# Attention in a perceiver block: narrow broadcast products for the inverse sums, and a minimum per chunk for the scores

## The chip, the cores and the metric

The kernel runs on one core of a Trainium2 chip. The metric is the device time of one execution in microseconds; the table below gives the median of several.

## What is computed

Cross attention with 16 heads of depth 32, then a quantised recurrent layer and a mixture of 8 experts, each on a layer-normalised input with a residual. The change lies in the attention:

```python
q = _split_heads(query_antecedent @ Wq, h) * d_head ** (-0.5)
k = _split_heads(memory_antecedent @ Wk, h)
v = _split_heads(memory_antecedent @ Wv, h)
logits = jnp.einsum('bhqd,bhkd->bhqk', q, k) + bias
weights = jax.nn.softmax(logits, axis=-1)
x = jnp.einsum('bhqk,bhkd->bhqd', weights, v)
```

There are 4 batches of 128 queries and 2048 keys, and one bias map of 128 x 2048 for all heads. The queries carry a factor of -1, so the kernel works with negated logits: it adds a negated bias, takes the least of each row, and raises exp(least - x).

## The kernel before, in words

Heads are worked in quads of four: quad n has batch n // 4, and four quads make a batch, counted here from the first to the fourth. A quad has eight slots, two per head. In a slot TensorE makes two score chunks of 128 x 512 (`score`, L482) in three PSUM banks used in turn (0, 1, 2), so a score waits until the addition three chunks before it has emptied its bank. VectorE empties it (`add_bias`, L712): one instruction adds the bias, writes the sum to `prob`, and keeps the row's minimum. The profile shows it as two rows, the custom instruction and a short one that reads the accumulator into `top`. The second to fourth chunk of a head start from the minimum of the chunk before, and so wait for it. After the fourth, ScalarE raises the whole head of 128 x 2048 to its exponential and sums it (`raise_head`, L894).

Two slots behind, TensorE transposes the exponentials of the quad before, by pairs of key tiles (`turn_pair`, L502, eight transposes a pair, banks 3 and 4 or 5 and 6 by turns). ScalarE copies most pairs out of PSUM (`move_pair`, L902), VectorE the rest (L722): pair 3 and 7 of a quad, and 6 in the third. Every second slot TensorE multiplies two finished pairs by the values (`multiply_pair`, L517), with products 32 columns wide that use four column tiles of its array. A transpose waits until the pair two before it, which had its banks, has been copied.

The order on each engine is written out by hand. On ScalarE the exponential of head j stands at the start of slot 2(j+1), ahead of that slot's copy. On VectorE in slot 3 stand `finish` (L746, the product of the attended values with the inverse sums of the quad two before) and `spread_sums` for the quad before; in slot 5, after its copy of a pair, `copy_sums`.

For the inverse sums VectorE takes reciprocals of the four sums (L728), repeats each 32 times into a 128 x 128 tile (L732), TensorE transposes that tile (`turn_sums`, L527), and VectorE copies it back (L738). The first quad of a batch runs beside the last projections of keys and values; after the fourth there is a tail with the remaining pairs and no scores, then the next batch's projections. GpSimd and the DMA queue of SyncE prepare the stacked keys of later heads.

The core of the addition before:

```python
if c:
    dve.wait_ge(*biased.at(n, j, c - 1))
dve.wait_ge(*scored.at(n, j, c))
dve.tensor_tensor_reduce(
    prob[:, slot, keys], psum[:, scores.of[n, j, c], :], biasmap[:, keys], 1.0,
    top[:, h, (c + 1) % 2:(c + 1) % 2 + 1] if c else HIGHEST, ALU.add, ALU.min,
    top[:, h, c % 2:c % 2 + 1]).then_inc(*biased.made(n, j, c))
```

Of the kernel before, what the change touches and what calls it, by code (L numbers as in the profile page):

```python
# [9 lines left out]
F32 = mybir.dt.float32  # L10
# [4 lines left out]
ALU = mybir.AluOpType  # L15
ACT = mybir.ActivationFunctionType
AX = mybir.AxisListType

P = 128
B = 4  # L20
D = 512
DT = D // P
KEYS = 2048
HEADS = 16
DH = D // HEADS
QUAD = P // DH
# [15 lines left out]
HIGHEST = 3.0e38  # L42
# [7 lines left out]
UNITS = KEYS // CHUNK  # L50
HALVES = 2
HALF = KEYS // HALVES
SLOTS_OF_QUAD = QUAD * HALVES
# [80 lines left out]
def perceiver_block(nc, a, out):  # L134
    with ExitStack() as life:
        def sb(name, shape, dt, stack=life):
            return stack.enter_context(nc.sbuf_tensor(name, shape, dt))
# [4 lines left out]
        def events(name, keys, by=1):  # L142
            return Events(sem(name), list(keys), by)

        psum = life.enter_context(nc.psum_tensor("psum", [P, 8, BANK], F32))


        ident = sb("ident", [P, P], F32)
        region_bias = ExitStack()
        biasmap = sb("biasmap", [P, KEYS], F32, region_bias)  # L150
# [17 lines left out]
        region_kv, region_f, region_r = ExitStack(), ExitStack(), ExitStack()  # L168
# [24 lines left out]
        prob = sb("prob", [P, PS, KEYS], F32, region_r)  # L193
        qstack = sb("qstack", [P, 2, QUAD, P], F32R, region_r)
        oT = sb("oT", [P, P], F32, region_r)
        probT = sb("probT", [P, 2, 2 * QUAD * P], F32, region_r)
        top = sb("top", [P, HEADS, 3], F32, region_r)
        rinv = sb("rinv", [P, 2, QUAD], F32, region_r)
        inverse = sb("inverse", [P, P], F32, region_r)
        region_r.close()  # L200
# [55 lines left out]
        def stack_landed(n, j):  # L256
# [28 lines left out]
        keys_high_g = events("keys_high_g", [(n, j) for n in quads if n % DT for j in range(QUAD)])  # L285
        keys_low_v = events("keys_low_v", [n for n in quads if n % DT == 0])
        keys_low_g = events("keys_low_g", [n for n in quads if n % DT])
        scored, biased = (events(name, [(n, j, c) for n in quads for j in range(QUAD) for c in range(UNITS)])
                          for name in ("scored", "biased"))
        raised = events("raised", [(n, j) for n in quads for j in range(QUAD)])  # L290
        def by_vector(n, p):

# [3 lines left out]
        turned, multiplied = events("turned", pairs), events("multiplied", pairs)  # L296
        moved_v = events("moved_v", [(n, p) for n, p in pairs if by_vector(n, p)])
        moved_a = events("moved_a", [(n, p) for n, p in pairs if not by_vector(n, p)])
        spread_out = events("spread_out", quads)
        sums_turned, sums_copied = events("sums_turned", quads), events("sums_copied", quads)  # L300
        weighted = events("weighted", quads)
        weights_summed = events("weights_summed", WINDOWS)
# [17 lines left out]
        def step_of_slot(n, i):  # L320

            t = SLOTS_OF_QUAD * (n % DT - 1) + i - TURN_LATER
            return t if t >= 0 else None
# [27 lines left out]
        def prob_slot(n, j):  # L351
            return (QUAD * n + j) % PS
# [47 lines left out]
        def tensor_attention(pe):  # L400
# [121 lines left out]
            def turn_sums(n):  # L522
                w, free = (scores.take(("sums", n), sums_copied.at(n)) if n < QUADS - 1 else
                           (2, scores.hold(2, ("sums", n), sums_copied.at(n))))
                pe.wait_ge(*spread_out.at(n))
                pe.wait_ge(*free)
                pe.transpose(psum[:, w, 0:P], inverse[:, :], ident[:, :]).then_inc(*sums_turned.made(n))  # L527

            def turn_and_weigh(b, t):
                turn_pair(*pair_of_step(b, t))  # L530
# [91 lines left out]
        def vector_attention(dve):  # L622
# [70 lines left out]

            def add_bias(n, j, c):
                b, g = divmod(n, DT)
                h, slot = QUAD * g + j, prob_slot(n, j)
                keys = slice(c * CHUNK, (c + 1) * CHUNK)
                if (n, j, c) == (0, 0, 0):
                    dve.wait_ge(*constants.at("bias"))
                    dve.wait_ge(*queries_stored.at(QUAD - 1, QUAD - 1))  # L700
                elif g == 0 and j == 0 and c == 0:
                    dve.wait_ge(*ternary_stored.at(b, 1))
                elif (g, j, c) == (1, 0, 0):
                    dve.wait_ge(*scored.at(n - 1, j, UNITS - 1))
                elif g >= 2 and j == 0:
                    dve.wait_ge(*(turned.at(n - 2, 2 * c + 1) if c else multiplied.at(n - 2, PAIRS // 2 - 1)))
                elif g >= 2 and (j, c) == (QUAD - 1, 0):
                    dve.wait_ge(*multiplied.at(n - 2, LAST))
                if c:
                    dve.wait_ge(*biased.at(n, j, c - 1))  # L710
                dve.wait_ge(*scored.at(n, j, c))
                dve.tensor_tensor_reduce(  # L712
                    prob[:, slot, keys], psum[:, scores.of[n, j, c], :], biasmap[:, keys], 1.0,
                    top[:, h, (c + 1) % 2:(c + 1) % 2 + 1] if c else HIGHEST, ALU.add, ALU.min,
                    top[:, h, c % 2:c % 2 + 1]).then_inc(*biased.made(n, j, c))

            def move_pair(n, p):
                w, free = pair_bank(p), turned_place_free(n, p)
# [3 lines left out]
                dve.tensor_copy(turned_pair(n, p), psum[:, w:w + 2, :].rearrange(  # L722
                    "p i (j q) -> p i j q", j=QUAD)).then_inc(*moved_v.made(n, p))

            def spread_sums(n):
                g = n % DT
                dve.wait_ge(*raised.at(n, QUAD - 1))
                dve.reciprocal(rinv[:, n % 2, :], top[:, QUAD * g:QUAD * (g + 1), 2]).then_inc(*own.made())  # L728
                dve.wait_ge(*own.last())
                if n >= 1:  # L730
                    dve.wait_ge(*weighted.at(n - 1))
                dve.tensor_copy(inverse[:, :].rearrange("p (j d) -> p j d", j=QUAD),  # L732
                                rinv[:, n % 2, :].rearrange("p (j d) -> p j d", d=1).broadcast_to([P, QUAD, DH])
                                ).then_inc(*spread_out.made(n))

            def copy_sums(n):
                dve.wait_ge(*sums_turned.at(n))
                dve.tensor_copy(inverse[:, :], psum[:, scores.of["sums", n], 0:P]).then_inc(*sums_copied.made(n))  # L738

            def finish(n):  # L740
# [57 lines left out]
            for b in range(B):  # L798
                for kind, c, i, tile in projected_tiles(b):
                    if kind == "values":  # L800
                        copy_value_tile(b, VTILES * c + i)
                    if b:
                        ternary_step(b, tile)
                    if (kind, i) == ("keys", DT - 1) and (b, c) != (0, 0):
                        split_chunk(CHUNKS * b + c + 1)
                    if (kind, c, i) == ("values", CHUNKS - 2, 0):
                        split_early_keys(b)
                    if b == 0 and (kind, c, i) == ("values", 0, 1):
                        split_query_weights()
                    if b == 0 and (kind, c, i) == ("values", 0, VTILES - 2):  # L810
                        split_rows()
                    if b == 0 and (kind, c, i) == ("values", 0, VTILES - 1):
                        split_chunk(1)
                        dve.wait_ge(*q_scaled.at(DT - 1))
                        split(q_hi.bitcast(F32R), q_lo.bitcast(F32R), q_all).then_inc(*parts_split.made("q"))
                split_first_keys(b)
                for n in range(DT * b, DT * (b + 1)):
                    for i in range(SLOTS_OF_QUAD):
                        j, half = divmod(i, HALVES)
                        for c in (2 * half, 2 * half + 1):  # L820
                            add_bias(n, j, c)
                        step = step_of_slot(n, i)
                        if step is not None and by_vector(*pair_of_step(b, step)):
                            move_pair(*pair_of_step(b, step))
                        if i == 3 and n > DT * b + 1:
                            finish(n - 2)
                        if i == 3 and n > DT * b:
                            spread_sums(n - 1)
                        if i == SUMS_AT and n > DT * b:
                            copy_sums(n - 1)  # L830
                last = DT * (b + 1) - 1
                if b == B - 1:
                    break
                move_pair(last - 1, LAST - 1)
                move_pair(last - 1, LAST)
                finish(last - 1)
                spread_sums(last)
                split_chunk(CHUNKS * (b + 1))
                copy_sums(last)
                move_pair(last, LAST)  # L840
                finish(last)
            return move_pair, spread_sums, copy_sums, finish, add_attention


        def scalar_attention(act):
# [43 lines left out]
                                   scale=1.0).then_inc(*made_ternary.made(b, p - 1))  # L889

            def raise_head(n, j):
                h, slot = QUAD * (n % DT) + j, prob_slot(n, j)
                act.wait_ge(*biased.at(n, j, UNITS - 1))
                act.activation(prob[:, slot, :], prob[:, slot, :], ACT.Exp, bias=top[:, h, 1:2], scale=-1.0,  # L894
                               accum_out=top[:, h, 2:3]).then_inc(*raised.made(n, j))

            def move_pair(n, p):
                w, free = pair_bank(p), turned_place_free(n, p)
# [589 lines left out]
            route(3)  # L1488


        def vector_recurrence(dve, move_pair, spread_sums, copy_sums, finish, add_attention):
            own = vector_own

            def prepare():
# [122 lines left out]
            move_tail(22)  # L1617
            move_tail(23)
            finish(last - 1)
            spread_sums(last)  # L1620
            add_attention(0)
            measure_x1(0)
            prepare()
# [1324 lines left out]
```

## Time and profile before

| | before |
|---|---|
| runs | 1007.76 us median of 3 (1007.1 to 1010.29) |
| the profiled execution | 1008.51 us, span 1006.7 us |
| TensorE clock granted over the span | 0.996 |
| busy: TensorE / VectorE / ScalarE / GpSimd | 97% / 61% / 49% / 26% |

The span is the time from the first to the last instruction; 1.8 us of the profiled execution lie around it. "Busy" of TensorE is modelled from starts and includes the latency of each product, so that a product that is late can still look busy. PE is TensorE, PEld its weight loads, DVE VectorE, ACT ScalarE, POOL GpSimd.

### The profile page before, as it was taken

To read this page: it belongs to the slowest core of one execution; us is meant where nothing else is said; L and a number is where in the kernel's file an instruction comes from. 1 tells how busy PE (TensorE), PEld (TensorE's weight loads), DVE (VectorE), ACT (ScalarE), POOL (GpSimd) and SP (SyncE) were. 2 spreads that over 40 slices of the span, in tenths; PEclk is the share of its full clock that TensorE was granted. 3 is DMA by queue.
4 is the path that set the end of the run, shared out by engine and by line. 5 is a ranking of instruction groups with operands and counts; after the bars stand their busy time and mean duration, and the time that the engine had idled before them with its cause. 6 is when DMAs were issued, how large, how long until landed. Compare 5 with 4: busy or idle time off the path is not lost. (4 is left out here: it accounts for less than half of the span.)

```text
span 1006.7 us, 18245 instructions
## 1 busy us (share of the span) xinstructions
PE 972.1 (97%) x7342; PEld 816.5 (81%) x7350; DVE 610.7 (61%) x1193; ACT 488.5 (49%) x633; POOL 263.0 (26%) x258
## 2 busy tenths in 40 slices
PE   9999999999999999999999999977899999999996
PEld 7888788888788888788888787654589999999995
DVE  6517895556895567886454885787852112455552
ACT  3211885171886055786151787578621102455551
POOL 2203830002830001840000850688400101111100
PEclk9999999999999999999999999999999999999998
DMA  8294861524761615771431778300079949699930
GB/s 292 71 190 86 178 151 48 209 88 122 176 163 49 274 42 177 173 188 49 160 101 42 176 161 298 125 1 1 33 266 380 373 157 341 218 381 351 345 100 13
DMA packets 77596, 169.92 MB, mean 169 GB/s; under 512 B 6472, under 2 KB 17608, under 8 KB 72384
## 3 DMA queue, kind: packets, MB, share of 16 engines
q1 hardware_dynamic: 75392, 163.87, 53.1%
q0 software_dynamic: 2112, 4.80, 2.0%
q8 instruction: 60, 0.98, 0.4%
q14 instruction: 32, 0.26, 0.1%
HBM read 119.01 MB, written 16.10 MB: 134 GB/s over the span
## 5 line engine op out<-in xcount | busy, mean ns | idle before, releaser
L995 POOL CAST stack<-kT 128x2048 fp32r<-128x2048 f32 x32 | 62.9, 1981 | 381.3 <-ACT kT L850 373.9
L712 DVE CUSTOM_DVE_ANT_0 prob<-psum,biasmap,top 128x512 f32<-128x512 f32 x192 | 144.2, 751 | 15.5 <-PE psum L482 7.0
L894 ACT ACTIVATE prob<-prob,top 128x2048 f32<-128x2048 f32 x64 | 128.6, 2010 | 37.7 <-DVE top L712 37.7
L2352 PE MATMUL psum<-xT,wring 128*128 128x128 f32 (+3 forms) x1024 | 134.0, 291 | 0.4 <-ACT xT L2706 0.4
L502 PE MATMUL psum<-ident,prob 128*128 128x128 f32 x1024 | 130.8, 274 | 1.3 <-ACT probT L902 1.3
L2352 PEld LDWEIGHTS psum<-xT,wring 128*128 128x128 f32 x1024 | 130.4, 191 | 1.8 <-ACT xT L2706 0.7
L502 PEld LDWEIGHTS psum<-ident,prob 128*128 128x128 f32 x1024 | 116.7, 140 | 16.0 <-issue 4.4
L850 ACT COPY kT<-psum 128x512 f32<-128x512 f32 x64 | 37.3, 585 | 189.1 <-PE psum L414 189.0
L429 PE MATMUL psum<-wv_hi,ctx_part 128*128 128x512 f32 x256 | 99.9, 390 | 0.1
L431 PE MATMUL psum<-wv_hi,ctx_part 128*128 128x512 f32 x256 | 99.6, 389 | 0.0
L430 PE MATMUL psum<-wv_lo,ctx_part 128*128 128x512 f32 x256 | 99.6, 389 | 0.0
L412 PE MATMUL psum<-ctx_part,wk_hi 128*128 128x512 f32 x240 | 94.2, 392 | 0.0
L413 PE MATMUL psum<-ctx_part,wk_hi 128*128 128x512 f32 x240 | 93.4, 389 | 0.0
L414 PE MATMUL psum<-ctx_part,wk_lo 128*128 128x512 f32 x240 | 93.4, 389 | 0.0
L666 DVE COPY v<-psum 128x512 f32<-128x512 f32 x48 | 32.8, 688 | 78.7 <-PE psum L431 78.7
L902 ACT COPY probT<-psum 128x1024 f32<-128x1024 f32 x64 | 63.4, 1008 | 18.5 <-PE psum L502 18.5
L2817 POOL DMA_INDIRECT out_x<-y_rows,row_id x11 | 17.0, 1545 | 208.4 <-DVE y_rows L2615 94.7
L2588 DVE TENSOR_SCALAR hidden<-psum,b 128x128 f32<-128x128 f32 (+3 forms) x64 | 23.5, 367 | 75.5 <-PE psum L2352 75.2
L2594 DVE TENSOR_TENSOR w_low<-wring,w_high 128x1024 fp32r<-128x1024 f32 x40 | 48.0, 1221 | 22.9 <-ACT w_high L2728 22.9
L2719 ACT ACTIVATE hidden<-psum,b 128x128 f32<-128x128 f32 (+3 forms) x64 | 24.4, 381 | 76.6 <-PE psum L2352 76.6
L2367 PE MATMUL psum<-hidden,wring 128*128 128x192 f32 (+2 forms) x384 | 58.0, 313 | 0.0
L2367 PEld LDWEIGHTS psum<-hidden,wring 128*128 128x128 f32 x384 | 57.3, 190 | 0.1
(285 smaller groups left out, 1789.8 us busy)
## 6 DMA issues: line engine op xcount, KB each, us to landing
wring<-in_w SPq DMA_DIRECT2D x64, 1024.0 KB, 8.5
ctx_raw<-in_ctx_t SPq DMA_DIRECT2D x15, 1024.0 KB, 6.2
stack<-stack SPq DMA_DIRECT2D x32, 256.0 KB, 4.7
early_stack<-early_stack SPq DMA_DIRECT2D x28, 256.0 KB, 4.0
prob<-in_w_gate_t SPq DMA_DIRECT2D x1, 5632.0 KB, 17.1
stack<-key_stack SPq DMA_DIRECT2D x20, 256.0 KB, 4.0
query_stacks<-prob SPq DMA_DIRECT2D x16, 256.0 KB, 5.4
qstack<-query_stacks SPq DMA_DIRECT2D x16, 256.0 KB, 5.2
```

The lines of the kernel that those rows point to most:

```text
L412: pe.matmul(psum[:, w, :], wh, ctx_part[:, half, 0, k, :], start=(k == 0), stop=False)
L413: pe.matmul(psum[:, w, :], wh, ctx_part[:, half, 1, k, :], start=False, stop=False)
L414: mm = pe.matmul(psum[:, w, :], wl, ctx_part[:, half, 0, k, :], start=False, stop=(k == DT - 1))
L429: pe.matmul(psum[:, w, :], ch, wv_hi[:, k, :], start=(k == 0), stop=False)
L430: pe.matmul(psum[:, w, :], ch, wv_lo[:, k, :], start=False, stop=False)
L431: mm = pe.matmul(psum[:, w, :], cl, wv_hi[:, k, :], start=False, stop=(k == DT - 1))
L502: mm = pe.transpose(psum[:, w + i, j * P:(j + 1) * P], prob[:, prob_slot(n, j), kt * P:(kt + 1) * P], ident[:, :])
L712: dve.tensor_tensor_reduce(prob[:, slot, keys], psum[:, scores.of[n, j, c], :], biasmap[:, keys], 1.0, top[:, h, (c + 1) % 2:(c + 1) % 2 + ...
L894: act.activation(prob[:, slot, :], prob[:, slot, :], ACT.Exp, bias=top[:, h, 1:2], scale=-1.0, accum_out=top[:, h, 2:3]).then_inc(*raised. ...
L902: act.copy(turned_pair(n, p), psum[:, w:w + 2, :].rearrange("p i (j q) -> p i j q", j=QUAD)).then_inc(*moved_a.made(n, p))
L2352: mm = pe.matmul(psum[:, w, 0:width], wring[piece][:, k, h % 4 * P:(h % 4 + 1) * P], xT[:, q % 2, k, 0:width], start=(k == 0), stop=(k == ...
L2367: mm = pe.matmul(y_place(q, k), wring[piece][:, h % 4, k * P:(k + 1) * P], hidden[:, h, 0:width], start=(h == 0), stop=(h == HT - 1))
```

## The change

It does three things.

- The inverse sums: VectorE no longer repeats the reciprocals. TensorE makes four products of 128 x 32 by 128 x 128 against the identity instead of one transpose, each with one column of `rinv` read 32 times as its weights, in the four column tiles.
- The additions: every chunk starts from the constant HIGHEST and keeps a minimum of its own, in a tile that is now indexed by slot; no addition waits for the one before.
- A small reduction of 128 x 4 on VectorE (`find_least`) finds the head's least. It stands behind the first addition of the next head, and for the fourth head of a quad right behind its last addition. The exponential waits for it.

```diff
-        top = sb("top", [P, HEADS, 3], F32, region_r)
+        top = sb("top", [P, 2 * QUAD, UNITS + 2], F32, region_r)
...
-                pe.wait_ge(*spread_out.at(n))
+                pe.wait_ge(*sums_inverted.at(n))
                 pe.wait_ge(*free)
-                pe.transpose(psum[:, w, 0:P], inverse[:, :], ident[:, :]).then_inc(*sums_turned.made(n))
+                for j in range(QUAD):
+                    mm = pe.matmul(psum[j * DH:(j + 1) * DH, w, 0:P], rinv[:, n % 2, j:j + 1].broadcast_to([P, DH]),
+                                   ident[:, :], start=True, stop=True, tile_position=(0, j * DH))
+                mm.then_inc(*sums_turned.made(n))
...
-                if c:
-                    dve.wait_ge(*biased.at(n, j, c - 1))
                 dve.wait_ge(*scored.at(n, j, c))
                 dve.tensor_tensor_reduce(
-                    prob[:, slot, keys], psum[:, scores.of[n, j, c], :], biasmap[:, keys], 1.0,
-                    top[:, h, (c + 1) % 2:(c + 1) % 2 + 1] if c else HIGHEST, ALU.add, ALU.min,
-                    top[:, h, c % 2:c % 2 + 1]).then_inc(*biased.made(n, j, c))
+                    prob[:, slot, keys], psum[:, scores.of[n, j, c], :], biasmap[:, keys], 1.0, HIGHEST, ALU.add,
+                    ALU.min, top[:, slot, c:c + 1]).then_inc(*biased.made(n, j, c))
+
+            def find_least(n, j):
+                slot = prob_slot(n, j)
+                dve.wait_ge(*biased.at(n, j, UNITS - 1))
+                dve.tensor_reduce(top[:, slot, UNITS:UNITS + 1], top[:, slot, 0:UNITS], AX.X,
+                                  ALU.min).then_inc(*biased.made(n, j, "least"))
...
-            def spread_sums(n):
-                g = n % DT
+            def invert_sums(n):
                 dve.wait_ge(*raised.at(n, QUAD - 1))
-                dve.reciprocal(rinv[:, n % 2, :], top[:, QUAD * g:QUAD * (g + 1), 2]).then_inc(*own.made())
-                dve.wait_ge(*own.last())
-                if n >= 1:
-                    dve.wait_ge(*weighted.at(n - 1))
-                dve.tensor_copy(inverse[:, :].rearrange("p (j d) -> p j d", j=QUAD),
-                                rinv[:, n % 2, :].rearrange("p (j d) -> p j d", d=1).broadcast_to([P, QUAD, DH])
-                                ).then_inc(*spread_out.made(n))
+                first = prob_slot(n, 0)
+                dve.reciprocal(rinv[:, n % 2, :], top[:, first:first + QUAD, UNITS + 1]).then_inc(*sums_inverted.made(n))
...
                         for c in (2 * half, 2 * half + 1):
                             add_bias(n, j, c)
+                            if j and c == 0:
+                                find_least(n, j - 1)
+                        if i == SLOTS_OF_QUAD - 1:
+                            find_least(n, j)
...
             def raise_head(n, j):
-                h, slot = QUAD * (n % DT) + j, prob_slot(n, j)
-                act.wait_ge(*biased.at(n, j, UNITS - 1))
-                act.activation(prob[:, slot, :], prob[:, slot, :], ACT.Exp, bias=top[:, h, 1:2], scale=-1.0,
-                               accum_out=top[:, h, 2:3]).then_inc(*raised.made(n, j))
+                slot = prob_slot(n, j)
+                act.wait_ge(*biased.at(n, j, "least"))
+                act.activation(prob[:, slot, :], prob[:, slot, :], ACT.Exp, bias=top[:, slot, UNITS:UNITS + 1],
+                               scale=-1.0, accum_out=top[:, slot, UNITS + 1:UNITS + 2]).then_inc(*raised.made(n, j))
```

VectorE's queue in the third quad of the first batch, from its copy of a pair in slot 1 to `finish` in slot 3; `ISA` with `prob,top` is the addition, `ISA top` its accumulator read, and the names in brackets are the events waited for. Before:

```order
L722 COPY prob<-psum 128x1024 [waits multiplied,turned]
L712 ISA prob,top<-psum,biasmap 128x512 [waits scored]
L712 ISA top 128x1
L712 ISA prob,top<-psum,biasmap,top 128x512 [waits scored,biased]
L712 ISA top 128x1
L712 ISA prob,top<-psum,biasmap,top 128x512 [waits scored,biased]
L712 ISA top 128x1
L712 ISA prob,top<-psum,biasmap,top 128x512 [waits scored,biased]
L712 ISA top 128x1
L746 TENSOR_TENSOR oT<-psum,inverse 128x128 [waits multiplied,sums_copied]
```

And now, at the same place:

```order
L733 COPY prob<-psum 128x1024 [waits multiplied,turned]
L718 ISA prob,top<-psum,biasmap 128x512 [waits scored]
L718 ISA top 128x1
L725 TENSOR_REDUCE top<-top 128x1 [waits biased]
L718 ISA prob,top<-psum,biasmap 128x512 [waits scored]
L718 ISA top 128x1
L718 ISA prob,top<-psum,biasmap 128x512 [waits scored]
L718 ISA top 128x1
L718 ISA prob,top<-psum,biasmap 128x512 [waits scored]
L718 ISA top 128x1
L753 TENSOR_TENSOR oT<-psum,inverse 128x128 [waits multiplied,sums_copied]
```

The reduction of the head before now stands behind this head's first addition, and the three waits on `biased` between additions are gone; the one left is the reduction's own.

TensorE's queue at the end of slot 5 of the second quad, between the products with the values and the next scores. Now (before, one row `L527 MATMUL psum<-ident,inverse 128x128` stood in place of the two of L533):

```order
L522 MATMUL psum<-probT,v 32x128 [waits moved_a]
L522 MATMUL psum<-probT,v 32x128 x7
L533 MATMUL psum<-ident,rinv 32x128 [waits biased,sums_inverted]
L533 MATMUL psum<-ident,rinv 32x128 x3
L487 MATMUL psum<-key_stack,qstack 128x512 [waits biased,stack4_in]
L487 MATMUL psum<-key_stack,qstack 128x512 [waits biased]
```

Four narrow products stand where one transpose stood; the neighbours are the same.

## Rows read from the trace of the kernel before

**Rows 1.** The page, costliest groups: the additions and the exponentials (busy us, mean ns; idle before).
```profile
L712 DVE CUSTOM_DVE_ANT_0 prob<-psum,biasmap,top 128x512 f32<-128x512 f32 x192 | 144.2, 751 | 15.5 <-PE psum L482 7.0
L894 ACT ACTIVATE prob<-prob,top 128x2048 f32<-128x2048 f32 x64 | 128.6, 2010 | 37.7 <-DVE top L712 37.7
```

**Rows 2.** TensorE's weight loads in time, third quad, first batch (start us, us; idle before).
```profile
129.04 0.19 PEld L482 LDWEIGHTS psum<-stack,qstack 128*128 128x128 f32 x1 [0.40 <-DVE top L712]
...
137.18 0.19 PEld L482 LDWEIGHTS psum<-key_stack,qstack 128*128 128x128 f32 x1 [0.35 <-DVE top L712]
```

**Rows 3.** TensorE in time, the same stretch.
```profile
128.47 1.07 PE L482 MATMUL psum<-stack,qstack 128*128 128x512 f32 x2
129.38 1.04 PE L502 MATMUL psum<-ident,prob 128*128 128x128 f32 x8
...
131.92 1.03 PE L502 MATMUL psum<-ident,prob 128*128 128x128 f32 x8
132.71 0.71 PE L482 MATMUL psum<-stack,qstack 128*128 128x512 f32 x2
133.26 1.03 PE L502 MATMUL psum<-ident,prob 128*128 128x128 f32 x8
134.23 1.08 PE L517 MATMUL psum<-probT,v 128*32 128x128 f32 x32
135.24 0.33 PE L527 MATMUL psum<-ident,inverse 128*128 128x128 f32 x1
135.32 0.72 PE L482 MATMUL psum<-key_stack,qstack 128*128 128x512 f32 x2
```

**Rows 4.** VectorE in time, third quad: slot 1's copy, then the next head.
```profile
127.16 1.22 DVE L722 COPY prob<-psum 128x1024 f32<-128x1024 f32 x1
128.30 0.68 DVE L712 CUSTOM_DVE_ANT_0 prob<-psum,biasmap 128x512 f32<-128x512 f32 x1
128.90 0.08 DVE L712 DVE_READ_ACCUMULATOR2_ANT top<- 128x1 f32 x1
129.02 0.75 DVE L712 CUSTOM_DVE_ANT_0 prob<-psum,biasmap,top 128x512 f32<-128x512 f32 x1
...
131.97 0.23 DVE L732 COPY inverse<-rinv 128x128 f32<-128x128 f32 x1
132.11 0.68 DVE L712 CUSTOM_DVE_ANT_0 prob<-psum,biasmap 128x512 f32<-128x512 f32 x1
```

**Rows 5.** VectorE, groups by shape (busy us, mean ns).
```profile
L712 DVE CUSTOM_DVE_ANT_0 prob<-psum,biasmap 128x512 f32<-128x512 f32 x64 | 43.9, 685 | 8.8 <-PE psum L482 7.9
L765 DVE TENSOR_REDUCE wmean<-psum 128x1 f32<-128x4 f32 x1 | 0.2, 152 | 0.0
```

**Rows 6.** VectorE in time, second quad: the change from head 0 to head 1.
```profile
111.60 0.75 DVE L712 CUSTOM_DVE_ANT_0 prob<-psum,biasmap,top 128x512 f32<-128x512 f32 x1
...
112.27 0.69 DVE L712 CUSTOM_DVE_ANT_0 prob<-psum,biasmap 128x512 f32<-128x512 f32 x1
```

**Rows 7.** ScalarE in time, third quad.
```profile
127.28 2.01 ACT L894 ACTIVATE prob<-prob,top 128x2048 f32<-128x2048 f32 x1 [1.01 <-DVE top L712]
...
129.28 0.99 ACT L902 COPY probT<-psum 128x1024 f32<-128x1024 f32 x1
```

**Rows 8.** ScalarE, then TensorE, in time: start of the second quad.
```profile
112.39 2.01 ACT L894 ACTIVATE prob<-prob,top 128x2048 f32<-128x2048 f32 x1 [1.06 <-DVE top L712]
...
114.40 1.90 ACT L902 COPY probT<-psum 128x1024 f32<-128x1024 f32 x2
...
115.44 1.09 PE L502 MATMUL psum<-ident,prob 128*128 128x128 f32 x8 [0.32 <-ACT probT L902]
```

**Rows 9.** ScalarE, then TensorE, in time: last quad and tail.
```profile
151.53 2.01 ACT L894 ACTIVATE prob<-prob,top 128x2048 f32<-128x2048 f32 x1 [0.86 <-DVE top L712]
...
153.54 0.99 ACT L902 COPY probT<-psum 128x1024 f32<-128x1024 f32 x1
...
155.80 1.97 PE L502 MATMUL psum<-ident,prob 128*128 128x128 f32 x16
```

More of the change, by code:

```diff
@@ L287, in perceiver_block, with chunks_and_least @@
         keys_low_g = events("keys_low_g", [n for n in quads if n % DT])
-        scored, biased = (events(name, [(n, j, c) for n in quads for j in range(QUAD) for c in range(UNITS)])
-                          for name in ("scored", "biased"))
+        def chunks_and_least(n, j):
+            before = [(n, j - 1, "least")] if j else []
+            after = [(n, j, "least")] if j == QUAD - 1 else []
+            return [(n, j, 0), *before, *((n, j, c) for c in range(1, UNITS)), *after]
+        scored = events("scored", [(n, j, c) for n in quads for j in range(QUAD) for c in range(UNITS)])
+        biased = events("biased", [key for n in quads for j in range(QUAD) for key in chunks_and_least(n, j)])
         raised = events("raised", [(n, j) for n in quads for j in range(QUAD)])
@@ L298, in perceiver_block @@
         moved_a = events("moved_a", [(n, p) for n, p in pairs if not by_vector(n, p)])
-        spread_out = events("spread_out", quads)
+        sums_inverted = events("sums_inverted", quads)
         sums_turned, sums_copied = events("sums_turned", quads), events("sums_copied", quads)
@@ L695, in add_bias @@
                 b, g = divmod(n, DT)
-                h, slot = QUAD * g + j, prob_slot(n, j)
+                slot = prob_slot(n, j)
                 keys = slice(c * CHUNK, (c + 1) * CHUNK)
@@ L723, in move_pair, with copy_sums @@
                     "p i (j q) -> p i j q", j=QUAD)).then_inc(*moved_v.made(n, p))
-            def spread_sums(n):
-                g = n % DT
+            def invert_sums(n):
                 dve.wait_ge(*raised.at(n, QUAD - 1))
-                dve.reciprocal(rinv[:, n % 2, :], top[:, QUAD * g:QUAD * (g + 1), 2]).then_inc(*own.made())
-                dve.wait_ge(*own.last())
+                first = prob_slot(n, 0)
+                dve.reciprocal(rinv[:, n % 2, :], top[:, first:first + QUAD, UNITS + 1]).then_inc(*sums_inverted.made(n))
+            def copy_sums(n):
+                dve.wait_ge(*sums_turned.at(n))
                 if n >= 1:
                     dve.wait_ge(*weighted.at(n - 1))
-                dve.tensor_copy(inverse[:, :].rearrange("p (j d) -> p j d", j=QUAD),
-                                rinv[:, n % 2, :].rearrange("p (j d) -> p j d", d=1).broadcast_to([P, QUAD, DH])
-                                ).then_inc(*spread_out.made(n))
-            def copy_sums(n):
-                dve.wait_ge(*sums_turned.at(n))
                 dve.tensor_copy(inverse[:, :], psum[:, scores.of["sums", n], 0:P]).then_inc(*sums_copied.made(n))
@@ L827, in vector_attention @@
                         if i == 3 and n > DT * b:
-                            spread_sums(n - 1)
+                            invert_sums(n - 1)
                         if i == SUMS_AT and n > DT * b:
@@ L836, in vector_attention @@
                 finish(last - 1)
-                spread_sums(last)
+                invert_sums(last)
                 split_chunk(CHUNKS * (b + 1))
@@ L841, in vector_attention @@
                 finish(last)
-            return move_pair, spread_sums, copy_sums, finish, add_attention
+            return move_pair, invert_sums, copy_sums, finish, add_attention
         def scalar_attention(act):
@@ L891, in raise_head @@
             def raise_head(n, j):
-                h, slot = QUAD * (n % DT) + j, prob_slot(n, j)
-                act.wait_ge(*biased.at(n, j, UNITS - 1))
-                act.activation(prob[:, slot, :], prob[:, slot, :], ACT.Exp, bias=top[:, h, 1:2], scale=-1.0,
-                               accum_out=top[:, h, 2:3]).then_inc(*raised.made(n, j))
+                slot = prob_slot(n, j)
+                act.wait_ge(*biased.at(n, j, "least"))
+                act.activation(prob[:, slot, :], prob[:, slot, :], ACT.Exp, bias=top[:, slot, UNITS:UNITS + 1],
+                               scale=-1.0, accum_out=top[:, slot, UNITS + 1:UNITS + 2]).then_inc(*raised.made(n, j))
             def move_pair(n, p):
@@ L1488, in tensor_recurrence, with vector_recurrence @@
             route(3)
-        def vector_recurrence(dve, move_pair, spread_sums, copy_sums, finish, add_attention):
+        def vector_recurrence(dve, move_pair, invert_sums, copy_sums, finish, add_attention):
             own = vector_own
@@ L1619, in vector_recurrence @@
             finish(last - 1)
-            spread_sums(last)
+            invert_sums(last)
             add_attention(0)
```

## The prediction

> **What bounds the kernel now.** I read three views, in this order: the page's groups, the waits in time on TensorE, and the three engines side by side in one quad. The groups show that VectorE's additions and ScalarE's exponentials carry the most work of their engines in the attention, and that the exponentials wait 37.7 us for VectorE [rows 1]. TensorE is the engine that counts: during the first quad of a batch its products follow one another without a gap, and in the tail too. In the other three quads it stops now and then. The reader is to see in the weight loads that the stop is a score that waits for its PSUM bank, 0.40 us at 129.04 and 0.35 us at 137.18 [rows 2]. In TensorE's own rows the two scores and the way to the next transposes take 0.91 us there (128.47 to 129.38), against 0.55 us where nothing waits (132.71 to 133.26) [rows 3]. So that stop costs 0.36 us, and the one at 137.18 by the same count 0.30 us.
>
> **What the change is worth on VectorE.** The first addition of a head, which starts from a constant, lasts 0.685 us, the other three 0.751 us [rows 1, 5]. Now all four start from the constant: 3 x 0.066 = 0.20 us less a head. The own waits: an addition that waits for the one before starts 0.12 us after the start of the accumulator read (128.90 to 129.02) [rows 4], while one that doesn't starts 0.67 us behind a long addition's start, which is where the read itself starts in rows 4 (0.60 us behind a short one, and long is 0.07 more) [rows 6]. So a wait is worth up to 0.12 us; since part of the gap may remain I take 0.05, together 0.15 us a head, with 0.35 as upper end. The reduction is new. A reduction of 128 x 4 took 152 ns [rows 5]; taken in full it costs 0.15 us a head. The copy that repeated the reciprocals goes, 0.14 us start to start [rows 4]. Net some 0.2 us of 3.1 a head go.
>
> What that buys on TensorE: the bank that 129.04 waited for was emptied by the addition at 128.30, which came late because four additions and the copy of 1.22 us at 127.16 stood ahead of it [rows 4]. That addition now starts 0.35 us earlier, 127.95, and the bank is free at 128.7, when TensorE asks for it. **The wait of 0.36 us goes**, and with VectorE ahead the 0.30 us go too. I find five such waits a batch: one in the second quad, two in each of the third and fourth. Two of the third quad are 0.66 us; with 0.36 for the second quad's that is 0.36 + 2 x 0.66, 1.7 us a batch, 6.8 us in all. That is the whole gain to be had.
>
> **What it costs on ScalarE.** The exponential of a head started at 127.28, as soon as its last addition was done [rows 7]. Now it waits for the reduction, and that stands behind the next head's first addition, which itself waits for a score of the next slot and for VectorE's copy of a pair. By the walk above this addition starts at 127.95, the reduction 0.6 us later, and with 0.15 us for it and 0.04 for the signal the exponential starts at 128.75: **1.4 to 1.5 us later**. Queued behind it on ScalarE is the copy at 129.28, which then starts at 130.75 and ends at 131.8. TensorE needs its banks for the transposes at 131.92 [rows 3, 7], now 0.36 us earlier since the stop is gone, so at 131.55. It waits 0.2 to 0.3 us. The next exponential was never early (ScalarE still has a copy to make), the third of the quad has the same delay as the first (it waited 0.83 us for VectorE before), and its copy is due at the next quad's first transposes: another 0.2. So a third or fourth quad loses 0.45 us to ScalarE and gains 0.66 us: 0.2 us better.
>
> The second quad has no slack to give. There the first exponential began at 112.39 right behind the addition of 111.60, its two copies ended at 116.3, and TensorE already waited for the first of them at 115.44 [rows 6, 8]. The reduction is now behind the addition of 112.27 as well: 112.27 - 0.05 + 0.60 + 0.19 = 113.0, so the exponential, both copies and those transposes move by 0.6 us. The stop of 0.36 us later in this quad goes, 0.2 of a new one comes: the second quad is 0.4 us worse. In the tail the copy at 153.54, which frees the banks for the transposes at 155.80, stands behind the exponential of 151.53 [rows 9]; that one is 1.5 us late, the copy ends at 156.1, and as the transposes are due at 155.6 TensorE waits 0.5 us.
>
> **What it costs on TensorE.** The transpose of the inverse took 0.08 us between its neighbours (135.24 to 135.32), though 0.33 us from start to end [rows 3]. The four products: 32 records of narrow products went by in 1.01 us (134.23 to 135.24), and a pair of key tiles needs 8 products, so two pairs are 16 products and each is two records [rows 3]. Four are 8 records, 0.25 us, 0.17 more than now; three times a batch in a slot 5, and once in the tail, where it is 0.1 to 0.2. In the last batch its neighbours are not narrow, and I add 0.25 for the switches there. Its lower end is 0, if the four go beside each other and beside what follows; its upper end takes each record at the pace of a full-width transpose, 0.79 us for eight (131.92 to 132.71) [rows 3]: 0.7 more for each of 16, 11 us. I take 0.17, by the row of the same shape. The Trainium skill, TensorEngine Tiling (Array Packing), Feature Incompatibilities, says that column tiling excludes the transpose mode for 32-bit input; the record counts agree, eight for eight transposes and two a product for the narrow ones. What reading one column 32 times as weights costs no row shows; I take it as the reading of 32 columns of `v` in those 32 records.
>
> **The sum.** Per batch: second quad +0.4, third and fourth 2 x -0.2, tail +0.5, narrow products 3 x 0.17 + 0.1 = 0.6: +1.1 less 0.1 for a shorter start of the second quad. Four batches 4.0, and 0.2 in the last: +4.2 us. Projections and the later layers follow TensorE and shift by the same. The profiled execution was 1008.5 us, so 1012.7 on its scale; it lies 0.75 us above the median, so I give **1011.9 us**. 0.3% of the time, 3 us, is about what a measurement tells from no change.
>
> **Rivals.**
> - *The exponentials have slack after all* (faster). If the copies' banks are needed later than I count, the five waits vanish and nothing takes their place. For it: in the third quad the copy that ended at 130.3 was needed at 131.9, 1.6 us of slack [rows 3, 7]. Against: the delay is 1.45 us and the need 0.36 us earlier, and the second quad had none. It decides if the exponential starts less than 1.2 us later, which the upper end of the own waits would bring near. Time: -6.8 + 2.6 for the narrow products = -4.2: 1003.6 us. Chance 0.13.
> - *The two cancel.* Each term is 0.2 to 0.6 us, and an error of 0.1 in the walk, met in 12 quads and 4 tails, is 1.6 us. With 0.12 us a wait instead of 0.05 VectorE is 0.2 us a head earlier still, the exponential starts at 128.5, and the new waits nearly halve: +1 to +2 us, 1009.3 us. Chance 0.3.
> - *The own waits gave nothing.* If the gap between additions stays, the walk has only 0.20 us a head: the addition of 128.30 starts 0.2 earlier, 0.15 of each old wait stays, and the exponential is 1.6 us late, 0.1 more for each new wait: +0.4 a batch, +5.8 us, 1013.5 us. Against it are the two starts of rows 4 and 6. The Trainium skill, VectorE: DVE Perf Modes, section on the drain that can't be avoided, says so: a semaphore between chained operations "costs nothing extra". By rows 4 and 6 it does cost something between an addition with its accumulator read and the next. Chance 0.17.
> - *The narrow products are slow* (a load of one repeated column, or a switch each time): 0.4 to 0.7 us each instead of 0.17, +8 to +12 us: 1018 us. Chance 0.05.
> - My forecast, 0.35.
>
> **The numbers.** The last three are slower by over 3 us, save a tail of the forecast: slower 0.53, same 0.32, faster 0.15. The range goes from 1004.5, which takes in the cancelling case and part of the first rival, to 1016.
>
> **What would show it.** In the profile after: additions all of 0.685 us; the waits of scores on the addition gone or under 0.1 us; 64 reductions of 0.15 us, with the exponentials waiting for them and starting 0.8 to 1.5 us behind their head's last addition; transposes that wait for ScalarE's copies, 0.2 to 0.3 us twice a quad, over 0.8 us at the start of the second quad, and 0.5 us in the tail; 128 records of narrow products at 0.03 us each. I'm wrong if the transposes don't wait for ScalarE.

## The result and the profile after

The changed kernel took 1010.75 us (median of 15 runs, 1010.03 to 1014.61), the kernel before beside it 1008.59 us (15 runs, 1006.81 to 1011.63). The ratio is 1.0024, 95% interval 1.0012 to 1.0035: slower by 2.4 us, between 1.2 and 3.5. That is clear of no difference, and mostly under the 3 us that I had set as the bound of "slower". The profiled execution spans 1009.2 us against 1006.7 before.

Runs of one kernel differ by the clock that was granted: of the 23 runs of the kernel before that stand beside the first four experiments, ten with a mean clock of 0.998 have a median of 1007.3 us, eight with 0.990 to 0.992 one of 1010.5 us. In the traces of all nine kernels the granted clock is 1.00 over the attention (94 to 640 us), so differences of one or two us are read there.

The costliest groups of the page, as in [rows 1], busy time, mean ns and idle before:

```profile
L718 DVE CUSTOM_DVE_ANT_0 prob<-psum,biasmap 128x512 f32<-128x512 f32 x256 | 168.0, 687 | 37.5 <-PE psum L487 33.9
L905 ACT ACTIVATE prob<-prob,top 128x2048 f32<-128x2048 f32 x64 | 128.8, 2012 | 49.2 <-DVE top L725 49.2
```

All 256 additions have the short form. VectorE's additions now wait 33.9 us for TensorE's scores (before 7.0 and 7.9 us for the two forms [rows 1, 5]), and the exponentials wait 49.2 us instead of 37.7. Who waited for whom in the attention (94 to 640 us), sums in us, times, longest:

```profile
PEld psum L507 <- ACT probT L913: 16.0, 27, 1.6
PE psum L507 <- ACT probT L913: 6.7, 8, 1.1
PEld psum L487 <- DVE top L718: 3.6, 5, 0.8
```

Before, the weight loads of scores waited 13.0 us for additions, 29 times, and those of transposes 2.6 us for ScalarE, 4 times. The waits have changed engine. The same stretch as in [rows 2, 3], first the weight loads that wait in the second to fourth quads and the tail of the first batch:

```profile
115.79 0.86 PEld L507 LDWEIGHTS psum<-ident,prob 128*128 128x128 f32 x8 [1.57 <-ACT probT L913]
123.77 0.87 PEld L507 LDWEIGHTS psum<-ident,prob 128*128 128x128 f32 x8 [0.20 <-ACT probT L913]
131.87 0.86 PEld L507 LDWEIGHTS psum<-ident,prob 128*128 128x128 f32 x8 [0.48 <-ACT probT L913]
139.96 0.14 PEld L507 LDWEIGHTS psum<-ident,prob 128*128 128x128 f32 x1 [0.31 <-ACT probT L913]
148.02 0.86 PEld L507 LDWEIGHTS psum<-ident,prob 128*128 128x128 f32 x8 [0.48 <-ACT probT L913]
156.10 1.77 PEld L507 LDWEIGHTS psum<-ident,prob 128*128 128x128 f32 x16 [0.81 <-ACT probT L913]
```

There is no score among them: the waits of 129.04 and 137.18 are gone. VectorE at the place of [rows 4], in time:

```profile
128.02 0.68 DVE L718 CUSTOM_DVE_ANT_0 prob<-psum,biasmap 128x512 f32<-128x512 f32 x1
128.63 0.09 DVE L718 DVE_READ_ACCUMULATOR2_ANT top<- 128x1 f32 x1
128.63 0.15 DVE L725 TENSOR_REDUCE top<-top 128x1 f32<-128x4 f32 x1
128.70 0.68 DVE L718 CUSTOM_DVE_ANT_0 prob<-psum,biasmap 128x512 f32<-128x512 f32 x1
129.30 0.08 DVE L718 DVE_READ_ACCUMULATOR2_ANT top<- 128x1 f32 x1
129.30 0.69 DVE L718 CUSTOM_DVE_ANT_0 prob<-psum,biasmap 128x512 f32<-128x512 f32 x1
```

Additions start 0.61 us apart, and 0.68 with the reduction between them: the reduction, 0.15 us long, costs VectorE 0.07. ScalarE at the place of [rows 7]:

```profile
128.82 2.02 ACT L905 ACTIVATE prob<-prob,top 128x2048 f32<-128x2048 f32 x1 [1.29 <-DVE top L725]
130.74 0.18 ACT L905 ACTIVATION_READ_ACCUMULATOR prob<-prob,top 128x1 f32 x1
130.82 1.90 ACT L913 COPY probT<-psum 128x1024 f32<-128x1024 f32 x2
```

The exponential starts at 128.82 where it started at 127.28, and the copies behind it at 130.82 where they started at 129.28. TensorE at the inverse sums:

```profile
134.23 1.08 PE L522 MATMUL psum<-probT,v 128*32 128x128 f32 x32
135.13 0.40 PE L533 MATMUL psum<-ident,rinv 128*32 128x128 f32 x8
135.46 0.73 PE L487 MATMUL psum<-key_stack,qstack 128*128 128x512 f32 x2
```

From the first product with the values to the next score: 1.23 us, before 1.09 (134.23 to 135.32 [rows 3]). The four narrow products cost 0.14 us more than the transpose. In the last batch, where their neighbours are full-width, it is more: from the transposes ahead of them to the product behind them 1.38 us (631.72 to 633.10), before 1.04 (630.30 to 631.34).

### The profile page after: what moved, and what is told of

It is laid out like the page before. It is cut to its first block, busy times and chain, and to the rows that moved or that the text cites. A ratio compares the mean times of both kernels' runs of the same rounds, so it can differ in the third digit from the quotient of the medians.

```text
span 1009.2 us, 18349 instructions
## 1 busy us (share of the span) xinstructions
PE 971.3 (96%) x7454; PEld 816.9 (81%) x7462; DVE 589.2 (58%) x1241; ACT 486.2 (48%) x633; POOL 262.8 (26%) x258
## 4 chain that ended last, share of the span: by engine, by line
PE 77%; DVE 6%; issue 5%; POOL 5%; ACT 4%; DMA 2%; POOLq 0%; ACTq 0%; DVEq 0%
PE psum L2363 10%; PE psum L507 9%; PE psum L2378 6%; PE psum L434 5%; PE psum L435 5%; PE psum L436 5%; PE psum L417 5%; PE psum L522 5%; PE psum L418 5%; PE psum L419 5%; PE psum L487 5%; DMA xg<-xm_rows,row_id 2%; PE psum L2395 2%; PE psum L2397 2%; PE psum L2396 2%
## 5 line engine op out<-in xcount | busy, mean ns | idle before, releaser
L718 DVE CUSTOM_DVE_ANT_0 prob<-psum,biasmap 128x512 f32<-128x512 f32 x256 | 168.0, 687 | 37.5 <-PE psum L487 33.9
L905 ACT ACTIVATE prob<-prob,top 128x2048 f32<-128x2048 f32 x64 | 128.8, 2012 | 49.2 <-DVE top L725 49.2
L507 PE MATMUL psum<-ident,prob 128*128 128x128 f32 x1024 | 131.8, 275 | 7.1 <-ACT probT L913 6.7
L507 PEld LDWEIGHTS psum<-ident,prob 128*128 128x128 f32 x1024 | 114.9, 140 | 28.8 <-ACT probT L913 16.0
L913 ACT COPY probT<-psum 128x1024 f32<-128x1024 f32 x64 | 61.3, 1006 | 10.9 <-PE psum L507 10.9
## 6 DMA issues: line engine op xcount, KB each, us to landing
prob<-in_w_gate_t SPq DMA_DIRECT2D x1, 5632.0 KB, 16.3
```

The costliest lines, as they stand in the source:

```text
L507: mm = pe.transpose(psum[:, w + i, j * P:(j + 1) * P], prob[:, prob_slot(n, j), kt * P:(kt + 1) * P], ident[:, :])
L718: dve.tensor_tensor_reduce(prob[:, slot, keys], psum[:, scores.of[n, j, c], :], biasmap[:, keys], 1.0, HIGHEST, ALU.add, ALU.min, top[:, s ...
```

## The experiments

Each was run in 5 rounds beside the kernel before; the ratios are to that kernel. The table sets beside them what the traces show of the attention alone: the time from the first score of the first batch to the same product of the recurrent layer behind the attention (640.91 in the trace before, 642.77 in the one after), and the waits of weight loads: those of scores for VectorE's additions and those of transposes for ScalarE's copies (94 to 640 us; times, us).

| kernel | attention, us | to before | scores for VectorE | transposes for ScalarE's copies |
|---|---|---|---|---|
| before | 547.0 | | 29, 13.0 | 4, 2.6 |
| the change | 548.8 | +1.8 | 5, 3.6 | 27, 16.0 |
| reduction at once | 543.2 | -3.7 | 13, 5.8 | 7, 4.7 |
| old sums | 546.4 | -0.6 | 5, 3.6 | 24, 15.4 |
| narrow products alone | 545.2 | -1.8 | 18, 8.6 | 7, 3.2 |
| at once, old sums | 541.9 | -5.1 | 18, 7.1 | 4, 4.1 |
| reduction later | 563.3 | +16.3 | 5, 3.6 | 27, 30.6 |
| copy ahead | 553.5 | +6.6 | 5, 3.6 | 11, 9.2 |
| own waits kept | 550.5 | +3.5 | 13, 5.4 | 27, 15.6 |

First one theory against two rivals. **A**: the exponentials start too late, and ScalarE's copies behind them hold the transposes. **B**: the narrow products carry the loss. **C**: the reduction loads VectorE too much wherever it stands.

### The reduction right behind its own head

The list that counts the events is changed to match, and left out here.

```diff
-                            if j and c == 0:
-                                find_least(n, j - 1)
-                        if i == SLOTS_OF_QUAD - 1:
-                            find_least(n, j)
+                            if c == UNITS - 1:
+                                find_least(n, j)
```

> The change, with the reduction of each head right behind the head's own last addition instead of behind the next head's first. Theory A (the late exponential on ScalarE is what costs): exponentials start about 0.3 us behind their last addition, the transposes' waits of 0.2 to 0.5 us for ScalarE's copies go in the third and fourth quads and the 0.54 us in the tail, the 1.13 us at the start of the second quad halves; about 1.5 us a batch less than the change, so 1004 to 1006 us. Theory B (the exponential's start does not matter, the narrow products carry the loss): 1010 to 1011.5 us, as the change. Theory C (the reduction itself loads VectorE too much, wherever it stands): scores wait for additions again, 1008 to 1010 us.

Measured: 1004.42 us, ratio 0.9948 (0.9932 to 0.9964). The one move turns a loss of 2.4 us into a gain of 5.2 us (in the attention +1.8 into -3.7). ScalarE in time, start of the second quad, then the third quad:

```profile
112.74 2.02 ACT L901 ACTIVATE prob<-prob,top 128x2048 f32<-128x2048 f32 x1 [1.05 <-DVE top L723]
...
127.20 2.01 ACT L901 ACTIVATE prob<-prob,top 128x2048 f32<-128x2048 f32 x1 [0.92 <-DVE top L723]
129.12 0.18 ACT L901 ACTIVATION_READ_ACCUMULATOR prob<-prob,top 128x1 f32 x1
129.21 0.99 ACT L909 COPY probT<-psum 128x1024 f32<-128x1024 f32 x1
```

The first batch starts 0.51 us later in this trace than before (its first score at 94.46 against 93.95), so the exponential of 127.20 is 0.6 us earlier than before. The waits in the attention:

```profile
PEld psum L485 <- DVE top L716: 5.8, 13, 0.8
PEld psum L505 <- ACT probT L909: 4.7, 7, 1.0
```

The 27 waits of transposes for ScalarE's copies are 7. B falls as the account of the whole loss, and C too: the products and the reduction are all still there. What the products cost by themselves is for the next runs.

### The inverse sums as before

```diff
-                for j in range(QUAD):
-                    mm = pe.matmul(psum[j * DH:(j + 1) * DH, w, 0:P], rinv[:, n % 2, j:j + 1].broadcast_to([P, DH]),
-                                   ident[:, :], start=True, stop=True, tile_position=(0, j * DH))
-                mm.then_inc(*sums_turned.made(n))
+                pe.transpose(psum[:, w, 0:P], inverse[:, :], ident[:, :]).then_inc(*sums_turned.made(n))
```

with the repeating copy of `spread_sums` on VectorE restored.

> The change, with the inverse sums as before (repeated on VectorE, one transpose). Theory A: the narrow products cost 0.14 us each on TensorE where it is full, so 1.7 to 2.5 us less than the change: 1008.5 us. Theory B: most of the loss is here, 1005 us or less. Were they hidden: 1010.7 us.

Measured: 1007.72 us, ratio 0.999 (0.9976 to 1.0003). Without the narrow products the rest of the change is no slower than the kernel before. The difference to the change is 0.34% of the time, 3.4 us by the two ratios, whose intervals are about 1.3 and 1.2 us either way. In the traces the attention of the two differs by 2.4 us (548.8 and 546.4), inside the 1.7 to 2.5 that I had counted. 15 times 0.14 and the last batch's 0.34 make the same, if the tails of the first three batches cost 0.14 as well.

### The narrow products alone

The same edit the other way, in the kernel before; its additions and exponentials are untouched.

> The kernel before with the narrow products alone, additions and exponentials untouched. Theory A: 16 times 0.1 to 0.2 us on TensorE less what VectorE's missing copy gives to the scores that wait, so +1 to +2 us: 1009.5 to 1010.5 us. Theory B: +2 us or more, all of the change's loss. If the missing copy on VectorE is worth more than the products cost: 1007 us.

Measured: 1007.02 us, ratio 0.9982 (0.9971 to 0.9994): 1.8 us faster. I had expected a loss, and had named this side only as the case in which the missing copy is worth more. A part of the ratio is the clock: nine of the 23 runs beside it had 0.994 or less, one of these 12 did, and among the runs at 0.998 the medians are 1007.0 (4 runs) and 1007.3 us (10 runs). The attention, at full clock in both traces, is 1.8 us shorter; that the whole kernel gains as much is not shown. The weight loads that wait in the third and fourth quads and in the tail, in time:

```profile
128.57 0.19 PEld L482 LDWEIGHTS psum<-stack,qstack 128*128 128x128 f32 x1 [0.39 <-DVE top L715]
129.88 0.81 PEld L517 LDWEIGHTS psum<-prob,v 128*32 128x32 f32 x32 [0.17 <-ACT probT L901]
137.87 0.81 PEld L517 LDWEIGHTS psum<-prob,v 128*32 128x32 f32 x32 [0.17 <-ACT probT L901]
144.69 0.19 PEld L482 LDWEIGHTS psum<-stack,qstack 128*128 128x128 f32 x1 [0.40 <-DVE top L715]
```

The wait at 129.04 has its counterpart at 128.57, the one at 137.18 is gone [rows 2], and so are its like in the second and fourth quad (120.91 and 153.49 before). VectorE fits that (third quad, from the reciprocal on):

```profile
131.31 0.17 DVE L731 RECIPROCAL rinv<-top 128x4 f32<-128x4 f32 x1
131.42 0.69 DVE L715 CUSTOM_DVE_ANT_0 prob<-psum,biasmap 128x512 f32<-128x512 f32 x1
```

From reciprocal to addition it is 0.11 us, with the repeated copy it was 0.34 (131.77 to 132.11). 0.23 us fewer ahead of the addition in slot 6, and a wait of 0.35 us does not arise. Three such waits a batch, of 0.3 to 0.4 us each, are some 4 us in all (the trace has 29 waits of 13.0 us before and 18 of 8.6 now); the products take back about 2.4 us (see above); an estimate of 1.6 to 2.0 is left, and 1.8 is what the attention shows. **So the sign of this part depends on how many waits for VectorE the missing copy takes away.** Here they are 11. In the change they are none (5 waits with the copy and 5 without it), and the products cost their whole 2.4 us.

### Both: reduction at once, sums as before

> Additions with own minimums, the reduction right behind the head's last addition, and the inverse sums as before. Theory A: both costs gone and the five waits for additions a batch still gone: 1002 to 1004 us, below both kernels by more than the measurement tells. Theory B: as the old sums alone. Theory C: 1006 to 1008 us.

Measured: 1003.72 us, ratio 0.9939 (0.992 to 0.9957): 6.1 us faster than the kernel before. The best of the study, below both kernels; by the intervals it can't be told apart from the version with the reduction moved alone (0.9948). The traces do tell them apart: the attention is 541.9 us here and 543.2 there, so the narrow products cost 1.4 us even where the exponentials are early. They take away 5 waits for VectorE there (18 to 13, 1.3 us), too few to pay for themselves.

### The reduction later still

```diff
-                            if j and c == 0:
+                            if j and c == 1:
                                 find_least(n, j - 1)
```

> The change, with the reduction one addition later still (behind the next head's second addition). Theory A: each exponential starts another 0.6 to 0.7 us later, in the third and fourth quads the two waits of transposes for ScalarE's copies grow by that much each (1.2 us a quad), the second quad's start and the tail by 0.6 us each and a wait of 0.6 us in between: 3 to 4 us a batch more, 1022 to 1027 us. If the exponentials had slack left: 1011 us, as the change.

Measured: 1026.0 us, ratio 1.0176 (1.0156 to 1.0195). The weight loads that wait from the second quad on:

```profile
116.41 0.86 PEld L507 LDWEIGHTS psum<-ident,prob 128*128 128x128 f32 x8 [2.18 <-ACT probT L913]
125.00 0.86 PEld L507 LDWEIGHTS psum<-ident,prob 128*128 128x128 f32 x8 [0.81 <-ACT probT L913]
133.68 0.86 PEld L507 LDWEIGHTS psum<-ident,prob 128*128 128x128 f32 x8 [1.08 <-ACT probT L913]
142.38 0.86 PEld L507 LDWEIGHTS psum<-ident,prob 128*128 128x128 f32 x8 [0.92 <-ACT probT L913]
151.06 0.86 PEld L507 LDWEIGHTS psum<-ident,prob 128*128 128x128 f32 x8 [1.09 <-ACT probT L913]
159.76 0.31 PEld L507 LDWEIGHTS psum<-ident,prob 128*128 128x128 f32 x3 [1.41 <-ACT probT L913]
```

The same six waits as in the change, each 0.60 or 0.61 us longer: 6 x 0.61 x 4 = 14.6 us. The attentions of the two traces differ by 14.5 us, and the two ratios by 1.5%, 15 us. Over this step of 0.61 us all that an exponential is later is paid in full, six times a batch.

### The copy ahead of the exponential

ScalarE's `raise_head` moved behind the `move_pair` of the same slot; the rest as in the change.

> The change, with ScalarE's copy of a slot ahead of the exponential where both stand in one slot. Theory A': only the copies' lateness costs, so with the copies free 1005 to 1007 us. Theory A (both the copies and the exponential are due, and whatever is second is late): the waits move to the first transposes of the quad and to the copy of the odd slot; 1011 to 1014 us.

Measured: 1015.52 us, ratio 1.0079 (1.006 to 1.0098). The theory that only the copies' lateness costs falls. TensorE and its weight loads in time:

```profile
112.99 1.10 PE L507 MATMUL psum<-ident,prob 128*128 128x128 f32 x8 [1.15 <-ACT prob L905]
...
118.09 1.09 PE L507 MATMUL psum<-ident,prob 128*128 128x128 f32 x8 [0.84 <-ACT probT L913]
...
128.92 0.86 PEld L507 LDWEIGHTS psum<-ident,prob 128*128 128x128 f32 x8 [0.52 <-ACT prob L905]
```

The first transposes of a quad now wait for the quad's last exponential, and the later ones for the copy that stands behind the next (beside the 11 waits for copies in the table there are 16 for exponentials, 10.7 us). Neither of the two orders on ScalarE takes up the late exponential; having its input early does. The result lies 1.5 us above my span.

### The own waits kept

```diff
+                if c:
+                    dve.wait_ge(*biased.at(n, j, c - 1))
                 dve.wait_ge(*scored.at(n, j, c))
```

> The change, with each addition again waiting for the one before, though it takes nothing from it. If a wait is worth 0.07 to 0.12 us on VectorE: additions start 0.73 us apart in place of 0.61, the exponentials of heads that follow back to back are up to 0.4 us later, 2 to 3 us more than the change: 1013 us. If the wait costs nothing (the vector page's rule): 1010.7 us and the starts unchanged at 0.61 us apart.

Measured: 1013.32 us, ratio 1.0046 (1.0028 to 1.0063), 2.2 us above the change by the ratios, with intervals that just overlap, and 1.7 us in the attention by the traces. The starts tell it more sharply than the time:

```profile
129.52 0.69 DVE L720 CUSTOM_DVE_ANT_0 prob<-psum,biasmap 128x512 f32<-128x512 f32 x1
130.14 0.08 DVE L720 DVE_READ_ACCUMULATOR2_ANT top<- 128x1 f32 x1
130.26 0.69 DVE L720 CUSTOM_DVE_ANT_0 prob<-psum,biasmap 128x512 f32<-128x512 f32 x1
130.87 0.08 DVE L720 DVE_READ_ACCUMULATOR2_ANT top<- 128x1 f32 x1
```

Additions start 0.73 to 0.74 us apart, against 0.61 in the change: a wait costs 0.12 us, as the starts in [rows 4] had it, though the instruction takes nothing from the one before. The Trainium skill, VectorE: DVE Perf Modes, "The DRAIN you can't avoid", says of eight chained copies, timed with a semaphore after each and after the last only, that "the semaphore costs nothing extra here"; for this instruction with its accumulator read the trace does not agree.

## Why the prediction was right, and where not

**The direction and the mechanism held.** I forecast +4.2 us, measured were +2.4 (1.2 to 3.5), 1.8 of them in the attention. The five waits of scores a batch that I counted as the whole gain are gone. The exponential of 127.28 was forecast at 128.75 and came at 128.82, and transposes wait for ScalarE in the places named: start of the second quad, twice in the third and fourth, tail. Moving the reduction forward takes these waits away and moving it back makes each of them longer, so they are shown to be its doing.

**That 128.82 meets the forecast of 128.75 is in part luck.** I had the addition ahead of it 0.35 us earlier than before (127.95) with waits worth 0.05 us. They are worth 0.12, which should have brought it forward further; it came at 128.02, only 0.28 us earlier, because VectorE was then stopped by TensorE, which the walk did not ask about:

```profile
123.92 0.69 DVE L718 CUSTOM_DVE_ANT_0 prob<-psum,biasmap 128x512 f32<-128x512 f32 x1 [1.15 <-PE psum L487]
...
126.27 0.69 DVE L718 CUSTOM_DVE_ANT_0 prob<-psum,biasmap 128x512 f32<-128x512 f32 x1 [0.30 <-PE psum L507]
```

The head's first addition waits for its score, and its fourth for transposes (L507) of the quad two before, which free the place in `prob` that it writes.

**The sizes, by the steps of the sum.** Before and after start the first batch 0.02 us apart, so the times can be set side by side.
- *Second quad, +0.4 less 0.1, and 0.17 for its products.* Its transposes came at 115.79 for 115.44, +0.35 us, not +0.6, and the third quad's first score at 123.27 for 123.23: +0.02 in all, where my terms make +0.47. Here the step failed. I had taken the own waits at 0.05 us, from a range up to 0.12, and the reduction at its full 0.15 us; they are 0.12 and 0.07, so the exponential began at 112.74 and not at 113.0.
- *Third and fourth quad, -0.2 each, and 0.17 for the products.* First score of the fourth quad at 139.35 for 139.50, so -0.2 net where I had -0.03: the same two terms. The waits for ScalarE that appear there (0.20, 0.48, 0.31, 0.48 us in the weight loads) look larger than what they cost: from the scores to the transposes behind them TensorE takes 0.57 us at 123.27, 0.78 at 131.09, 0.61 at 139.35 and 0.78 at 147.24, where 0.57 or 0.58 is the way without a stop. The second of each quad costs 0.2 us, as forecast, the first 0.04 or less; a quad loses some 0.2 us to ScalarE where I had 0.45.
- *Tail, +0.5 and 0.1.* The transposes of 155.80 came at 156.11, though the products ahead of them were 0.30 us earlier (154.49 for 154.79), so the stop is 0.6 us: as forecast for the tail. The next batch begins 0.43 us late in all (247.32 for 246.87, less the 0.02), where my sum had 1.0.
- *Narrow products, 0.17 each.* 0.14 measured, and 0.34 in the last batch where I had 0.17 and 0.25 for switches. The load that reads one column 32 times shows no price: 128 loads of 110 ns on average, where those of `v` took 109.

The first three batches lose 0.43, 0.30 and 0.38 us, the last one 0.73: 1.84 us in all (640.91 to 642.77 for the same product of the recurrence in both traces, less the 0.02). The other 0.6 us of the spans' difference arises behind the attention; the change does not touch anything there, no run looked for it, and its cause stays open.

**The rivals.** That the two effects cancel was the nearest rival, with "0.12 us a wait instead of 0.05" as its condition and +1 to +2 us as its price. That condition is what was measured, and the time lies between that rival and the forecast; but its mechanism did not follow, for the exponential was to start at 128.5 and started at 128.82. That the own waits give nothing is refuted by the starts, the slow narrow product by the 0.14 us. That the exponentials have slack is refuted by the waits of transposes and by the run with the reduction later.

**What I missed** is not in the sum at all: the missing copy on VectorE. I booked it as 0.14 us of VectorE's time, and said nothing of the narrow products' worth by themselves. In the kernel before they shorten the attention by 1.8 us; with the reduction at once they lengthen it by 1.4, and in the change by 2.4.

## What to carry to other kernels

When a step is moved to spare a queue a wait (here the reduction, behind the next head's first addition), ask what the consumer then waits for in addition: the next slot's score, a copy and an addition stood in between, and the exponential came 1.5 us later, to save VectorE one own wait of 0.12. Where three engines run this close to each other, count which waits of the bound engine a trade between them removes before pricing it: the same edit made the attention 1.8 us shorter where it removed 11 waits, 1.4 us longer where it removed 5, and 2.4 us longer where it removed none. And walk the queue behind the late instruction: it was the copies behind the exponential, not the exponential, that TensorE missed, yet putting them ahead of it cost 5 us more.

## What was not expected of the hardware

- A reduction of 128 x 4 that takes 0.15 us lengthens the way between two additions by 0.07 us only, where it does not wait for the one just ahead: it runs beside the accumulator read (both start at 128.63), and the next addition starts 0.07 us into it.
- The wait between two additions costs 0.12 us even where the awaited value is not used.
- Weights read from one column 32 times cost no more than others: the four products went by in 0.33 us, the way back to the full-width scores included (135.13 to 135.46), and their loads are as long as those of `v`.
